# A four-stage local attention layer on one core: three groups of matmuls in another place of TensorE's order

## The chip, the cores and the metric

The kernel runs on one core of one Trainium2 chip. The metric is the device time of one execution in microseconds. A core has five engines that run their own instruction streams and meet through semaphores: TensorE (PE in the profile, with its weight loads as PEld), VectorE (DVE), ScalarE (ACT), GpSimd (POOL) and SyncE (SP), which issues the DMAs.

## What is computed

The reference is `x + attention(xn) * silu(ffn(xn))` on 4096 tokens of 256 features, with `xn` the normalised input. The change lies in the second branch, which applies two layers of this kind (cut to its attention half; each layer then has a gated MLP):

```python
h = shift_token(x)                       # second half of the features from the token before
q, k, v = split(h @ wqkv)                # 8 heads of 64
q = l2norm(q) * qs;  k = l2norm(k) * ksc
q, k = rotary_xpos(q, k)                 # rotation with a position-dependent scale
o = local_attention(q, k, v)             # windows of 128, each sees itself and the one before
x = x + o @ wo
```

## The kernel before, in words

The program goes through stages one after the other: projection and global attention (to about 1700 us of the trace), its output product, then for each of two layers `local_attention_layer` and `mlp_layer`, and a final gate. Only `local_attention_layer` is touched. It runs twice, the first time from about 1745 to 2312 us of the trace, the second from about 2581 to 3149 us.

**The pipeline.** The 32 windows are taken in 16 pairs (`NI = 16`). Every engine runs the same loop `for k in range(NI + 4)`, and in iteration k works on pairs of different age; `live(k)` is true for the pairs 0 to 15, `win(w)` for the windows 0 to 31. The order inside an iteration is written out by hand on every engine. Since each engine executes in its own order, an instruction that waits holds all behind it on that engine. Iterations 4 to 15 have all work; iterations 16 to 19 are the drain, in which nothing new is projected.

On PE one iteration of before is, in this order (lines of the profile):

- `score_max(2k-3)` (L1142): scores of a window, from which DVE takes the row maxima (`row_max`, L1350, eight custom reductions of 128x256)
- transposes of X for pair k (L1260)
- `weigh(k-4, 1)` (L1245): the softmax weights PT times V, and times ones for the sums, heads 4 to 7; DVE then divides (`divide`: reciprocal L1382, product L1386), ACT copies the high part (L1071), POOL takes the low part (L992)
- `score_turned(2k-5)` (L1159 for the maxima, L1166 for the scores): the transposed scores, of which ACT makes exponentials (L1043, `weights`), and POOL cuts the corners (L1001, L1005, `trim`)
- transposes of the norm factors (L1276), which DVE multiplies into the rotated q and k of pair k-1 (L1420)
- `turn_max(2k-3)` (L1180): the maxima transposed into bank B7, copied by ACT to `negm` (L1051)
- `values(2k)` (L76 to L78 into B6): 6 matmuls of 512 columns; ACT copies them to V (L1058)
- **the output product of pair k-4** (L76 to L78 with `a_woh`, `a_oTh`, also into B6): 24 matmuls of 256 columns; DVE adds it to X (L1428)
- `project(k, 0)` and `project(k, 1)` (L76 to L78 into BP): 12 matmuls each; ACT squares them (L1064), DVE rotates them (`turn`, L1376)
- `score_max(2k-2)`, `project(k, 2)`, `project(k, 3)`, `values(2k+1)`, `score_turned(2k-4)`
- sums of squares into B6 (L1313), copied by ACT to `sse` (L1117)
- `turn_max(2k-2)` (L1180)
- **the sums of squares transposed** (L1321, two transposes into B6); DVE takes them (L1440, `ssc`), POOL raises them to the power -1/2 (L1026), ACT spreads them (L1096, `rnx`)
- `weigh(k-3, 0)` (L1245): heads 0 to 3 of the pair before.

`product3` writes each fp32 product as three matmuls of high and low parts, which is why the lines L76, L77 and L78 come in turn.

**Buffers that tie the order.** B6 is shared by the value products, the output product, the sums of squares and the sums of `weigh(p, 1)`; B7 by the transposed maxima, the transposes of X and the sums of `weigh(p, 0)`. So `weigh(p, 0)` waits until ACT has copied the maxima out of B7, and `weigh(p, 1)` waits until DVE has read the output product before it and `ssc` out of B6:

```python
                if q == 0:
                    ...
                    pe.wait_ge(nm_done, min(2 * k - 1, NT))
                else:
                    pe.wait_ge(ssc_done, min(k + 1, NI))
                    if p >= 1:
                        pe.wait_ge(x2_done, p)
```

## Time and profile before

| | |
|---|---|
| median of 3 runs | 3445.2 us (3440.74 to 3447.95) |
| profiled execution, its own time | 3442.12 us |
| span of that execution | 3440.4 us |
| mean granted TensorE clock | 0.954 of full speed |
| PE busy | 3080.8 us (90% of the span) |
| PEld busy | 1909.2 us (55%) |
| DVE busy | 2413.1 us (70%) |
| ACT busy | 1714.0 us (50%) |
| POOL busy | 953.9 us (28%) |
| first local layer's iterations | about 1745 to 2312 us of the span |
| second local layer's iterations | about 2581 to 3149 us of the span |

A row of a timeline gives the start in us from the span's start, the duration in us, the engine, the line and operation, what is written and read, and how many instructions were merged. In square brackets stands how long the engine was idle before it and what ended that. Merged matmuls overlap their neighbours, since they are pipelined; the distance between starts tells more than a duration. The PEclk column is the granted clock of TensorE, where 1.00 is 2.4 GHz and 0.50 is 1.2 GHz.

### The profile page before, as it was taken

How to read it: one execution, taken by the hardware profiler on the slowest of the kernel's cores; microseconds unless marked ns; L12 is line 12 of the kernel's file. 1: busy time of each engine (PE TensorE's matmuls, PEld its weight loads, DVE VectorE, ACT ScalarE, POOL GpSimd, SP SyncE). 2: the span in 40 equal slices, each digit the busy share in tenths (PEclk: the TensorE clock that was granted, in tenths of full speed). 3: DMA queues.
4: the chain of work that ended last, by engine and by line, in shares of the span. 5: the costliest groups of instructions: out<-in, count | busy, mean ns of one | idle time of the engine just before them, and what ended most of it. 6: DMA issues, size and time to landing. Idle time of an engine off the chain costs nothing. (4 is left out here: it accounts for less than half of the span.)

```text
span 3440.4 us, 77045 instructions
## 1 busy us (share of the span) xinstructions
PE 3080.8 (90%) x31756; PEld 1909.2 (55%) x31756; DVE 2413.1 (70%) x4236; ACT 1714.0 (50%) x3173; POOL 953.9 (28%) x1011
## 2 busy tenths in 40 slices
PE   7799999999999999999868998968987999986996
PEld 6333333334443333434457777757876777765875
DVE  7699999987889997875246666645555666664555
ACT  5267777887778888887223333322223333332222
POOL 8410000000110000001035545532224555542223
PEclk9699999999999999999789999989998999998998
DMA  8420001000020000000220000000000000003001
GB/s 255 127 63 17 9 9 46 9 9 18 25 69 17 9 9 10 5 8 8 73 91 20 20 14 20 32 28 6 0 5 31 20 16 19 20 26 112 0 0 49
DMA packets 61014, 113.91 MB, mean 33 GB/s; under 512 B 9240, under 2 KB 25368, under 8 KB 60056
## 3 DMA queue, kind: packets, MB, share of 16 engines
q1 hardware_dynamic: 56600, 103.07, 9.6%
q10 hardware_dynamic: 4096, 6.30, 0.7%
q8 instruction: 236, 3.87, 0.5%
q14 instruction: 82, 0.67, 0.1%
HBM read 75.00 MB, written 33.55 MB: 32 GB/s over the span
## 5 line engine op out<-in xcount | busy, mean ns | idle before, releaser
L650 DVE TENSOR_REDUCE mp<-ps_m 128x2 f32<-128x1024 f32 (+3 forms) x1152 | 1275.8, 1134 | 192.5 <-PE ps_m L701 134.8
L628 ACT ACTIVATE probs<-ps_s 128x512 f32<-128x512 f32 (+3 forms) x2304 | 1162.1, 561 | 380.5 <-PE ps_s L725 349.7
L741 PE MATMUL ps_o<-probs,vall 128*32 128x256 f32 (+3 forms) x9216 | 711.1, 380 | 15.4 <-POOL probs L605 9.1
L725 PE MATMUL ps_s<-qst,kst 64*128 64x512 f32 (+3 forms) x2304 | 595.7, 486 | 4.3 <-ACT probs L628 2.9
L701 PE MATMUL ps_m<-kst,qst 64*128 64x512 f32 (+3 forms) x2304 | 481.3, 401 | 33.1 <-DVE mp L650 15.7
L725 PEld LDWEIGHTS ps_s<-qst,kst 64*128 64x128 f32 x2304 | 241.3, 187 | 459.3 <-ACT probs L628 398.9
L741 PEld LDWEIGHTS ps_o<-probs,vall 128*32 128x32 f32 x9216 | 186.0, 109 | 342.1 <-issue 177.0
L701 PEld LDWEIGHTS ps_m<-kst,qst 64*128 64x128 f32 x2304 | 233.3, 192 | 77.1 <-DVE mp L650 57.8
L594 POOL TENSOR_TENSOR msplit<-negm,mzero 128x16 fp32r<-128x16 f32 x32 | 7.2, 224 | 907.0 <-DVE negm L656 907.0
L1020 POOL TENSOR_TENSOR a_rot<-a_scr 128x512 f32<-128x512 f32 x128 | 163.4, 1277 | 321.3 <-DVE a_scr L1376 321.3
L605 POOL TENSOR_SCALAR_AFFINE_SELECT probs<-probs 128x256 f32<-128x256 f32 x256 | 103.0, 406 | 513.0 <-ACT probs L628 512.9
L1554 ACT ACTIVATE m_gl<-m_bank_u,m_b 128x512 f32<-128x512 f32 x96 | 66.0, 688 | 346.7 <-PE m_bank_u L78 346.7
L1376 DVE SCALAR_TENSOR_TENSOR a_scr<-a_BP,a_sc,a_tab 128x256 f32<-128x256 f32 x384 | 167.5, 478 | 63.5 <-ACT a_scr L1064 63.2
L1064 ACT ACTIVATE a_scr<-a_BP 128x512 f32<-128x512 f32 x128 | 76.5, 598 | 266.7 <-PE a_BP L78 266.7
L1350 DVE CUSTOM_DVE_ANT_0 a_SU<-a_SU,a_mask 128x256 f32<-128x256 f32 (+1 forms) x512 | 196.5, 459 | 9.8 <-issue 9.8
L1071 ACT ACTIVATE a_oTh<-a_on 128x512 fp32r<-128x512 f32 x64 | 40.4, 631 | 317.0 <-DVE a_on L1386 317.0
L1026 POOL TENSOR_TENSOR a_rn<-a_ssc,a_half 128x32 f32<-128x32 f32 x32 | 174.1, 5441 | 40.5 <-DVE a_ssc L1440 40.5
L76 PE MATMUL m_bank_u<-m_hh,Wh 128*128 128x512 f32 x384 | 155.7, 405 | 31.5 <-DVE m_uf L1663 31.5
L1382 DVE RECIPROCAL a_rec<-a_B 128x256 f32<-128x256 f32 x64 | 112.2, 1753 | 98.3 <-PE a_B L1245 98.1
L1537 POOL TENSOR_TENSOR m_ul<-m_uf,m_uh 128x512 fp32r<-128x512 f32 x96 | 126.2, 1314 | 195.4 <-DVE m_uh L1669 195.4
L1043 ACT ACTIVATE a_PT<-a_SU 128x1024 f32<-128x1024 f32 (+1 forms) x128 | 121.8, 1003 | 89.2 <-PE a_SU L1166 89.2
L78 PE MATMUL m_bank_u<-m_hh,Wl 128*128 128x512 f32 x384 | 152.9, 398 | 0.0
(189 smaller groups left out, 5411.7 us busy)
## 6 DMA issues: line engine op xcount, KB each, us to landing
a_tab<-in_rope SPq DMA_DIRECT2D x32, 512.0 KB
q_parts<-pparts SPq DMA_DIRECT2D x32, 256.0 KB, 3.6
k_parts<-pparts SPq DMA_DIRECT2D x32, 256.0 KB, 3.9
qst<-q_parts SPq DMA_DIRECT2D x64, 128.0 KB, 2.7
o_raw<-o_sb SPq DMA_DIRECT2D x32, 256.0 KB, 2.0
X<-in_x SPq DMA_DIRECT2D x8, 512.0 KB, 5.7
kst<-k_parts SPq DMA_DIRECT2D x32, 128.0 KB, 3.7
qst<-q_parts SPq DMA_DIRECT2D x64, 64.0 KB, 2.6
```

What stands on the lines that cost most here:

```text
L76: pe.matmul(out, a_hi, b_hi, start=start, stop=False)
L78: return pe.matmul(out, a_lo, b_hi, start=False, stop=stop)
L628: act.activation(probs[:, s % PR, h, off:C], sslots[n % SR][:, off:C], ACT.Exp, scale=float(D) ** -0.5).then_inc(exp_done, 1)
L650: dve.tensor_reduce(mp[b % 2][:, h:h + 2, cc:cc + 1], slot[:, :, 0:width], AX.X, ALU.max).then_inc(max_read, 1)
L701: last = pe.matmul(slot[:, x, 0:width], qst[q_slot(b)][rows, hp, a * P:(a + 1) * P], kst[g % 2][rows, hp, cc * C:cc * C + width], start=Tr ...
L725: pe.matmul(sslots[n % SR][:, off:C], kst[g % 2][rows, hp, i * P:(i + 1) * P], qst[q_slot(b)][rows, hp, off:C], start=True, stop=True).the ...
L741: last = pe.matmul(ps_o[32 * h:32 * h + VW, lo:hi], vall[:, i, (g * GH + h) * DV:(g * GH + h) * DV + VW], probs[:, s % PR, h, lo:hi], star ...
L1020: pool.tensor_tensor(rot[:, g, :, :].rearrange("p a b -> p (a b)"), t[:, n % 2, 0, :, :].rearrange("p a b -> p (a b)"), t[:, n % 2, 1, :, ...
L1026: pool.tensor_tensor(rn[:, :, :, :].rearrange("p a b c -> p (a b c)"), ssc[:, :, :, :].rearrange("p a b c -> p (a b c)"), half[:, :], ALU. ...
L1350: dve.tensor_tensor_reduce(SU[:, i, q * N2 + lo:(q + 1) * N2], SU[:, i, q * N2 + lo:(q + 1) * N2], mask[:, lo:N2], 1.0, -3.0e38, ALU.add, ...
L1376: dve.scalar_tensor_tensor(out=dst, in0=src, scalar=s, in1=table, op0=ALU.mult, op1=ALU.mult).then_inc(rope_done, 1)
L1537: pool.tensor_tensor(u_lo[:, m, :], uf[:, m % 2, :], u_hi[:, m, :].bitcast(F32), ALU.subtract).then_inc(ul_done, 1)
```

## The change

Three groups are moved; no instruction is added or removed, and no wait is changed but by its place.

1. **Output product in the iterations that project** (k = 4 to 15): on PE it moves from behind `values(2k)` to behind `project(k, 0)`. Its code becomes the helper `project_out(p)`. DVE's order stays.
2. **Sums of squares transposed**: the two transposes (L1321) move from before `weigh(k-3, 0)` to behind it. DVE's order stays: `ssc`, then the division of `weigh(k-3, 0)`.
3. **Output product in the drain** (k = 16 to 19): on PE it moves from the middle of the iteration to its end, behind `weigh(k-3, 0)`; on DVE the addition to X moves to the end of the iteration, behind `divide(k-3, 0)`.

```diff
--- before.py
+++ after.py
@@ -1247,6 +1247,21 @@
                                              tile_position=(0, 32 * i), skip_group_check=True)
                 last.then_inc(av_done, 1)
 
+            def project_out(p):
+                if live(p):
+                    if p == 0:
+                        pe.wait_ge(wl_done, 1)
+                    pe.wait_ge(olo_done, 2 * p + 2)
+                    pe.wait_ge(rec_done, 2 * p + 2)
+                    if live(p + 4):
+                        pe.wait_ge(vc_done, 2 * (p + 4) + 1)
+                    for a in range(2):
+                        tok = slice(a * P, (a + 1) * P)
+                        for j in range(OC):
+                            last = product3(pe, B6[:, a * E:(a + 1) * E], oT_hi[:, j, tok], oT_lo[:, j, tok], wo_hi[:, j, :],
+                                            wo_lo[:, j, :], j == 0, j == OC - 1)
+                    last.then_inc(wo_done, 1)
+
             for k in range(NI + 4):
                 if win(2 * k - 3):
                     score_max(2 * k - 3)
@@ -1280,22 +1295,9 @@
                     turn_max(2 * k - 3)
                 if live(k):
                     values(2 * k)
-                if live(k - 4):
-                    p = k - 4
-                    if p == 0:
-                        pe.wait_ge(wl_done, 1)
-                    pe.wait_ge(olo_done, 2 * p + 2)
-                    pe.wait_ge(rec_done, 2 * p + 2)
-                    if live(k):
-                        pe.wait_ge(vc_done, 2 * k + 1)
-                    for a in range(2):
-                        tok = slice(a * P, (a + 1) * P)
-                        for j in range(OC):
-                            last = product3(pe, B6[:, a * E:(a + 1) * E], oT_hi[:, j, tok], oT_lo[:, j, tok], wo_hi[:, j, :],
-                                            wo_lo[:, j, :], j == 0, j == OC - 1)
-                    last.then_inc(wo_done, 1)
                 if live(k):
                     project(k, 0)
+                    project_out(k - 4)
                     project(k, 1)
                 if win(2 * k - 2):
                     score_max(2 * k - 2)
@@ -1315,13 +1317,15 @@
                     last.then_inc(ss_done, 1)
                 if win(2 * k - 2):
                     turn_max(2 * k - 2)
+                if live(k - 3):
+                    weigh(k - 3, 0)
                 if live(k):
                     pe.wait_ge(sse_done, k + 1)
                     for a in range(2):
                         last = pe.transpose(B6[:, a * P:(a + 1) * P], sse[:, a * P:(a + 1) * P], id_sb[:, :])
                     last.then_inc(sst_done, 1)
-                if live(k - 3):
-                    weigh(k - 3, 0)
+                else:
+                    project_out(k - 4)
 
         @block.vector
         def _(dve):
@@ -1386,6 +1390,12 @@
                     dve.tensor_tensor(on[:, 2 * q:2 * q + 2, :], BP[q][:, :, :],
                                       rec[:, q, :].rearrange("p (o n) -> p o n", o=1).broadcast_to([P, 2, N2]), ALU.mult
                                       ).then_inc(on_done, 1)
+
+            def add_out(p):
+                if live(p):
+                    dve.wait_ge(wo_done, p + 1)
+                    xt = X[:, 2 * p:2 * p + 2, :].rearrange("p a e -> p (a e)")
+                    dve.tensor_tensor(xt, B6[:, :], xt, ALU.add).then_inc(x2_done, 1)
 
             for k in range(NI + 4):
                 if k == 1:
@@ -1421,12 +1431,8 @@
                                           rot[:, 2 * b:2 * b + 2, :, :],
                                           BP[b][:, :, :].rearrange("p g (o n) -> p g o n", o=1).broadcast_to([P, 2, 2, N2]),
                                           ALU.mult).then_inc(nrm_done, 1)
-                if live(k - 4):
-                    p = k - 4
-                    dve.wait_ge(wo_done, p + 1)
-                    xt = X[:, 2 * p:2 * p + 2, :].rearrange("p a e -> p (a e)")
-                    dve.tensor_tensor(xt, B6[:, :], xt, ALU.add).then_inc(x2_done, 1)
-                if live(k):
+                if live(k):
+                    add_out(k - 4)
                     turn(k, 0)
                     turn(k, 1)
                 if win(2 * k - 2):
@@ -1440,6 +1446,8 @@
                     dve.tensor_scalar(ssc[:, :, :, :], B6[:, 0:N2].rearrange("p (a g c) -> p a g c", a=2, g=4)[:, :, :, 0:4],
                                       1e-24, None, ALU.max).then_inc(ssc_done, 1)
                 divide(k - 3, 0)
+                if not live(k):
+                    add_out(k - 4)
 
 
 def mlp_layer(nc, layer, X, W, w_next, ahead, w_2, b_1, ln_cols, b_2, ident, shift, carry):
```

How the orders differ at three places; the names are those of the profile, with the buffer's number where it tells two apart.

PE, first iteration with an output product, from the value product (into B6, operand `Wh`, `a0_hTh`) on. Before, the output product (`a0_woh`, `a0_oTh`) follows:

```order
L76 MATMUL a0_B6<-Wh,a0_hTh 128x512
L77 MATMUL a0_B6<-Wl,a0_hTh 128x512
L78 MATMUL a0_B6<-Wh,a0_hTl 128x512
L76 MATMUL a0_B6<-a0_woh,a0_oTh 128x256
L77 MATMUL a0_B6<-a0_wol,a0_oTh 128x256
L78 MATMUL a0_B6<-a0_woh,a0_oTl 128x256
```

With the change the quarter of the projection (into BP0) comes first; its last three rows and the output product's first three:

```order
L76 MATMUL a0_BP0<-a0_hTh,Wh 128x256
L77 MATMUL a0_BP0<-a0_hTl,Wh 128x256
L78 MATMUL a0_BP0<-a0_hTh,Wl 128x256
L76 MATMUL a0_B6<-a0_woh,a0_oTh 128x256
L77 MATMUL a0_B6<-a0_wol,a0_oTh 128x256
L78 MATMUL a0_B6<-a0_woh,a0_oTl 128x256
```

The 24 matmuls of the output product stand one quarter, 12 matmuls, later than before.

PE, end of an iteration. Before: maxima transposed, sums of squares transposed (`a0_sse`), weighting (`a0_PT`), scores of the next iteration (`a0_SU`):

```order
L1180 MATMUL a0_B7<-a0_id,a0_msp 128x128 x2
L1321 MATMUL a0_B6<-a0_id,a0_sse 128x128 x2
L1245 MATMUL a0_BP0<-a0_PT,a0_V 32x128 x4
L1245 MATMUL a0_BP0<-a0_PT,a0_V 32x256 x4
L1245 MATMUL a0_BP0<-a0_PT,a0_V 32x128 x8
L1245 MATMUL a0_BP0<-a0_PT,a0_V 32x256 x4
L1245 MATMUL a0_BP0<-a0_PT,a0_V 32x128 x4
L1245 MATMUL a0_B7<-a0_PT,a0_ones 32x128 x4
L1245 MATMUL a0_B7<-a0_PT,a0_ones 32x256 x4
L1245 MATMUL a0_B7<-a0_PT,a0_ones 32x128 x4
L1142 MATMUL a0_SU<-a0_QK 128x256 x16
```

With the change:

```order
L1180 MATMUL a0_B7<-a0_id,a0_msp 128x128 x2
L1245 MATMUL a0_BP0<-a0_PT,a0_V 32x128 x4
L1245 MATMUL a0_BP0<-a0_PT,a0_V 32x256 x4
L1245 MATMUL a0_BP0<-a0_PT,a0_V 32x128 x8
L1245 MATMUL a0_BP0<-a0_PT,a0_V 32x256 x4
L1245 MATMUL a0_BP0<-a0_PT,a0_V 32x128 x4
L1245 MATMUL a0_B7<-a0_PT,a0_ones 32x128 x4
L1245 MATMUL a0_B7<-a0_PT,a0_ones 32x256 x4
L1245 MATMUL a0_B7<-a0_PT,a0_ones 32x128 x4
L1325 MATMUL a0_B6<-a0_id,a0_sse 128x128 x2
L1142 MATMUL a0_SU<-a0_QK 128x256 x16
```

The two transposes now stand behind the whole weighting and before the next scores (the trace counts 72 matmuls of a weighting, where these rows add up to 36).

DVE, drain, iterations 17 and 18 from the division of `weigh(13, 1)` on (`Wl` is the low part of the MLP's weights). Before:

```order
L1382 RECIPROCAL a_rec<-a_B 128x256
L1386 TENSOR_TENSOR a_on<-a_BP,a_rec 128x512
L1428 TENSOR_TENSOR X<-a_B,X 128x512
L1382 RECIPROCAL a_rec<-a_B 128x256
L1386 TENSOR_TENSOR a_on<-a_BP,a_rec 128x512
L1397 TENSOR_TENSOR Wl<-a_scr,Wh 128x3072
L1382 RECIPROCAL a_rec<-a_B 128x256
L1386 TENSOR_TENSOR a_on<-a_BP,a_rec 128x512
L1428 TENSOR_TENSOR X<-a_B,X 128x512
```

With the change:

```order
L1386 RECIPROCAL a_rec<-a_B 128x256
L1390 TENSOR_TENSOR a_on<-a_BP,a_rec 128x512
L1386 RECIPROCAL a_rec<-a_B 128x256
L1390 TENSOR_TENSOR a_on<-a_BP,a_rec 128x512
L1398 TENSOR_TENSOR X<-a_B,X 128x512
L1407 TENSOR_TENSOR Wl<-a_scr,Wh 128x3072
L1386 RECIPROCAL a_rec<-a_B 128x256
L1390 TENSOR_TENSOR a_on<-a_BP,a_rec 128x512
L1386 RECIPROCAL a_rec<-a_B 128x256
L1390 TENSOR_TENSOR a_on<-a_BP,a_rec 128x512
L1398 TENSOR_TENSOR X<-a_B,X 128x512
```

The addition to X now follows the second division of its iteration, and `Wl` follows it directly.

## Rows read from the trace of the kernel before

**Rows 1.** Windows of the first local layer, steady part and drain; busy us, then PEclk
```profile
1850.00:2250.00 400.00, 363.06 (x5410) 295.31 (x5410) 265.30 (x770) 132.32 (x218) 218.42 (x187) 1.00 0.07 20
2250.00:2313.00 63.00, 42.66 (x764) 35.27 (x756) 26.80 (x54) 13.65 (x17) 18.28 (x20) 0.86 0.01 2
```
**Rows 2.** Waits of PE over the whole span: total us, times, longest
```profile
PE a_B L1321 <- ACT a_sse L1117: 28.3, 30, 1.0
...
PE a_B L76 <- POOL a_oTl L992: 28.0, 8, 6.3
...
PE a_B L76 <- ACT a_V L1058: 25.7, 24, 1.1
```
**Rows 3.** Timeline of PE, one pair in the steady part: start us, duration us, what
```profile
2049.17 0.40 PE L78 MATMUL a_B<-Wh,a_hTl 128*128 128x512 f32 x1
...
2050.64 0.35 PE L76 MATMUL a_B<-a_woh,a_oTh 128*128 128x256 f32 x1 [1.07 <-ACT a_V L1058]
...
2053.56 0.28 PE L76 MATMUL a_BP<-a_hTh,Wh 128*128 128x256 f32 x1
...
2056.53 2.07 PE L1142 MATMUL a_SU<-a_QK 32*128 32x128 f32 x64
```
**Rows 4.** Timeline of DVE, the same stretch
```profile
2053.76 0.69 DVE L1428 TENSOR_TENSOR X<-a_B,X 128x512 f32<-128x512 f32 x1 [4.26 <-PE a_B L78]
```
**Rows 5.** Timeline of ACT, the same pair and the start of the next
```profile
2049.89 0.61 ACT L1058 ACTIVATE a_V<-a_B 128x512 f32<-128x512 f32 x1
...
2067.61 0.41 ACT L1051 ACTIVATE a_negm<-a_B 128x256 fp32r<-128x256 f32 x1
...
2074.66 1.04 ACT L1096 ACTIVATE a_rnx<-a_rn 128x1024 f32<-128x1024 f32 x1
```
**Rows 6.** Timeline of PE, end of that pair
```profile
2067.79 0.44 PE L1321 MATMUL a_B<-a_id,a_sse 128*128 128x128 f32 x2 [0.97 <-ACT a_sse L1117]
...
2068.16 1.94 PE L1245 MATMUL a_BP<-a_PT,a_V 128*32 128x128 f32 x48
...
2070.90 2.01 PE L1142 MATMUL a_SU<-a_QK 32*128 32x256 f32 x32
```
**Rows 7.** Timeline of ACT, then of PE, end of the first drain iteration
```profile
2259.98 0.39 ACT L1051 ACTIVATE a_negm<-a_B 128x256 fp32r<-128x256 f32 x1
...
2260.51 1.94 PE L1245 MATMUL a_BP<-a_PT,a_V 128*32 128x128 f32 x48 [1.81 <-ACT a_negm L1051]
```
**Rows 8.** Timeline of DVE, end of that pair
```profile
2068.27 0.19 DVE L1440 TENSOR_SCALAR a_ssc<-a_B 128x32 f32<-128x32 f32 x1 [2.57 <-PE a_B L1321]
...
2071.04 1.76 DVE L1382 RECIPROCAL a_rec<-a_B 128x256 f32<-128x256 f32 x1 [2.58 <-PE a_B L1245]
```
**Rows 9.** Timeline of PE, first part of the next pair
```profile
2076.66 0.44 PE L1159 MATMUL a_SU<-a_negm,a_rowso 32*128 32x128 f32 x8 [0.41 <-DVE a_mx L1350]
...
2079.10 0.66 PE L1276 MATMUL a_BP<-a_id,a_rnx 128*128 128x128 f32 x4
```
**Rows 10.** Timeline of POOL, the same stretch
```profile
2068.54 5.45 POOL L1026 TENSOR_TENSOR a_rn<-a_ssc,a_half 128x32 f32<-128x32 f32 x1 [1.49 <-DVE a_ssc L1440]
```
**Rows 11.** Timeline of PE, last three iterations of the first local layer
```profile
2279.20 1.95 PE L1245 MATMUL a_BP<-a_PT,a_V 128*32 128x128 f32 x48
...
2292.28 0.58 PE L76 MATMUL a_B<-a_woh,a_oTh 128*128 128x256 f32 x1 [6.34 <-POOL a_oTl L992]
...
2297.22 1.95 PE L1245 MATMUL a_BP<-a_PT,a_V 128*32 128x128 f32 x48
...
2299.85 1.92 PE L1245 MATMUL a_BP<-a_PT,a_V 128*32 128x128 f32 x48
```
**Rows 12.** Timeline of POOL, the same iterations
```profile
2276.66 0.63 POOL L1005 TENSOR_SCALAR_AFFINE_SELECT a_PT<-a_PT 128x512 f32<-128x512 f32 x1
...
2293.36 1.22 POOL L1001 TENSOR_SCALAR_AFFINE_SELECT a_PT<-a_PT 128x512 f32<-128x512 f32 x2
```
**Rows 13.** Timeline of DVE, the same iterations
```profile
2284.49 3.35 DVE L1397 TENSOR_TENSOR Wl<-a_scr,Wh 128x3072 fp32r<-128x3072 f32 x1
```

## The prediction

> **What bounds the kernel now.** I first looked at the windows, to see whether the touched stage is short of TensorE or of something else. In the steady part of the first local layer PE is busy 363 of 400 us at full clock, while DVE has 265 and the others less; in the drain PE is busy 42.7 of 63 us, at a mean clock of 0.86 [rows 1]. So in the steady part time is gained by closing holes in PE, and in the drain by shortening chains. The list of PE's waits names the holes that the change aims at: 25.7 us in 24 waits of the output product for ACT's copy of the values, 28.3 us in 30 waits of the turned sums of squares for ACT's `sse`, 28.0 us in 8 waits of the output product for POOL's low part [rows 2]. Taken at their names that is 82 us. The timelines, read next, show that only the first is what it seems. Both layers run the same instructions at the same distances, so I count one and double.
>
> **Part 1, the output product behind a quarter of the projection.** The last value matmul starts at 2049.17, the output product at 2050.64 after 1.07 us of idleness, the projection at 2053.56, the next scores at 2056.53 [rows 3]. The product thus takes 2.92 us and a quarter of the projection 1.49 (half of 2.97). The quarter needs neither B6 nor ACT's copy, so it starts when the values end, some 0.3 us after 2049.17. It ends at about 2050.9, the copy at 2049.89 + 0.61 = 2050.50 [rows 5], so the product no longer waits. The scores then start 0.3 + 1.49 + 2.92 + 1.49 = 6.2 us after 2049.17 instead of 7.36: 1.2 us earlier. Does DVE allow it? Its addition to X starts at 2053.76, 0.20 behind the product's end [rows 4], and comes 0.2 to 0.3 us later now; but the rotation behind it, which had to wait for the first quarter's squares, finds them ready, and starts over 1 us earlier. Iterations 4 to 15 of two layers are 24 cases: 24 x 1.2 = 28.8 us less. Bounds: the printed idleness alone gives 25.7, a start without any gap 29.5.
>
> **Part 2, the turned sums of squares behind the weighting.** PE idles 0.97 us before these transposes (2067.79), and the weighting follows at 2068.16 [rows 6]. That wait looks free to take. But the weighting writes its sums into B7 and so needs ACT's copy of the maxima, which runs from 2067.61 to 2068.02 [rows 5]. The weighting starts 0.14 us after that. In the drain, where nothing stands between, the copy ends at 2260.37 and the weighting starts at 2260.51, again 0.14 later [rows 7]. So the weighting is held by the copy already, will start at the same time, and the idleness before it only grows from 0.97 to about 1.34 us. Gain: nothing. The cost: the transposes now stand at the weighting's end, where the next scores started, 2070.90 [rows 6]. PE's scores move back by 0.37 (2067.79 to 2068.16). DVE took `ssc` 0.48 us after the transposes' start, at 2068.27, and started the reciprocal at 2071.04 [rows 8]. Now `ssc` starts at 2070.90 + 0.48 = 2071.38, lasts 0.19, and the reciprocal, queued behind it on DVE, starts at about 2071.55: 0.5 us later. Behind it are the product, eight maxima and their split; PE waits for exactly these at 2076.66, by 0.41 us [rows 9]. DVE sets the pace there, so 0.5 us is paid in full. The weighting of a pair and the projection of a new one fall together in iterations 3 to 15, twice: 26 x 0.5 = 13.0 us more. Bounds: 0.37 each (PE's share alone) gives 9.6, 0.48 + 0.19 = 0.67 each gives 17.4. One more queue has to bear it: POOL's power -1/2, 5.45 us long, started 0.27 us after `ssc` [rows 10] and comes 3.1 us later, to end at 2077.1; ACT's spreading (1.04 us, [rows 5]) ends at 2078.2. PE wants it at 2079.10 + 0.5 [rows 9]. That leaves 1.4 us of slack: cost nothing.
>
> Here the clock has to be looked at. In the steady part holes of 1.07 and 0.97 us recur in every iteration, and the granted clock stays at 1.00 [rows 1, 3, 6]; so a hole of 1.34 us instead of 0.97, with the 1.07 gone, is costed at nothing. The Trainium skill (TensorE: Matmul & The Clock Gate, section on HAM oscillation) says that matmul groups separated by waits can each start at the low clock, every time anew. By that rule the sum would be some 50 us higher (worked out below as a rival), and I do not take it, since this trace holds its clock through such holes.
>
> **Part 3, the drain.** Before, the output product waits up to 6.34 us for the low part, then runs from 2292.28 to 2297.22, 4.94 us instead of 2.92 because PE idled before it: the low clock costs 2.0 us [rows 3, 11]. Moving it behind the weighting hides these waits, but `weigh(p, 1)` of the next iteration may only start when the addition to X has emptied B6, and this now stands behind weighting and product in a line. Followed through: the weighting of pair 14 is held by POOL's trims, which end at 2277.29, so it starts at 2277.4 instead of 2279.20 [rows 11, 12]. Weighting 2.74, product 2.92, addition 0.20 + 0.69: done at 2284.0. Only then comes `Wl` on DVE, 3.35 us [rows 13], done at 2287.3 where it was 2287.84: the chain division, high part, low part, trims behind it gains 0.5 us, and the weighting of pair 15, which waits for the trims (before: to 2294.58, [rows 12]), starts at 2294.1 instead of 2297.22 [rows 11]. PE has idled for 6 us by then, so I give the weighting 2.74 + 2.0. Product and addition: 2302.7. Then `weigh(15, 1)` starts, where before it started at 2299.85. From there the chain to the layer's end is as before. The drain gets longer by 2.8 us per layer, 5.6 together. The first two drain iterations give back what they gain, since the product that leaves one row of scores comes before the next. Bounds: 0 per layer, if the weighting keeps the full clock and some gain survives; 5, if one more burst falls to the low clock.
>
> **Sum.** -28.8 + 13.0 + 5.6 = -10.2 us. The profiled execution took 3442.1 us and would take 3431.9. The median of the runs is 3445.2, 3.1 above it, so the prediction is 3435.0. The ends: -29.5 + 9.6 + 0 = -19.9 gives 3425.3; -25.7 + 17.4 + 10 = +1.7 gives 3446.9.
>
> **The rivals.**
> - *The wait for `sse` does vanish.* Then the weighting starts 1.3 us earlier, the reciprocal 0.8: -28.8 - 26 x 0.8 + 5.6 = -44, 3401 us. For it speaks the list of waits, which names `sse` 28.3 us; against it the 0.14 us in both places [rows 5 to 7]. 0.03.
> - *The drain gains.* The last product of a layer keeps its wait; if the other six lose theirs and nothing takes their place, 28.0 x 6/8 = 21 us go: -28.8 + 13.0 - 21 = -36.8, 3408 us. Against it speaks the wait on `x2_done`. 0.06.
> - *The norm factors come late.* If POOL's power ends later than I make it, by trims or low parts before it in its queue, PE waits at L1276. It decides from 1.4 us of further delay; each 0.1 us beyond costs 2.6 us in 26 cases. With 0.3 us it is 3443. 0.10.
> - *The clock falls before the weighting, and the kernel gets slower.* The place is the hole of 1.34 us in front of L1245. A burst at 1.2 GHz costs 2.0 us more (4.94 against 2.92). In all 26 cases: 3435 + 52 = 3487 us; from 5 bursts on the gain is gone, from 9 on the kernel is slower by over 0.2%. This is the rule of the Trainium skill named above (TensorE: Matmul & The Clock Gate). 0.05.
> - *The value copy is not covered after all*, with only some 0.3 us between its end and the product's new place, or the drain is worse than its bound: 3440 to 3450. 0.04.
>
> **Chances and range.** The forecast's own case has 0.72, spread over 3427 to 3443. A measurement of this kernel can tell about 0.2% (6.9 us) from no change. Faster by more, below 3438.3: 0.60 of the forecast's 0.72, the two fast rivals (0.09) and 0.02 of the third, 0.71. Within: 0.11 of the forecast, 0.07 of the third rival and 0.03 of the last, 0.21. Slower: 0.01 of the forecast, 0.05 of the clock and 0.02 of the others, 0.08. The range 3422 to 3443 leaves out the two fast rivals (0.09), the clock, and a few hundredths at the upper end.
>
> **What would show it.** In the profile after: no wait of the output product for `a_V`, the next scores 6.2 us after the last value matmul. PE idle about 1.3 us before the weighting, released by `negm` (L1051), still 0.14 us behind its end; `ssc` and the reciprocal adjacent on DVE, the latter 3.4 us after the weighting's start where it was 2.9. The distance of equal points in neighbouring iterations 0.7 us shorter than before. In the drain the 6.34 us wait for POOL gone, but `weigh(15, 1)` waiting for the addition to X, and the layer's last addition some 3 us later counted from the last `sse`. I am wrong if the weighting starts earlier relative to the copy, if L1276 waits for `rnx` in the steady part, or if the clock there leaves 1.00.

## The result, and the profile after

The median of 15 runs is 3454.3 us (3448.7 to 3463.0), that of the kernel before, run beside it, 3440.8: a ratio of 1.0043 with an interval of 1.0033 to 1.0052. The change makes the kernel 13.5 us slower, which is more than the 6.9 us that the prediction called measurable, and the time lies above the predicted range of 3422 to 3443 us. The profiled execution is the slowest of the fifteen, 3463.0 us, 20.9 above the profiled one of before.

The list of PE's waits (total us, times, longest) shows that the waits which the change aims at did go:

```profile
PE a_BP L1245 <- ACT a_negm L1051: 39.0, 28, 2.1
PE a_BP L1291 <- DVE a_on L1390: 31.5, 26, 1.3
...
PE a_BP L1245 <- POOL a_PT L1001: 12.2, 2, 6.1
...
PE a_B L76 <- POOL a_oTl L992: 9.2, 2, 4.6
...
PE a_SU L1159 <- ACT a_negm L1051: 5.6, 2, 2.8
...
PE a_BP L1245 <- DVE X L1398: 3.5, 4, 0.9
...
PE a_B L1325 <- ACT a_sse L1117: 2.9, 4, 1.0
```

The 25.7 us for `a_V` are gone from the output product, the 28.3 us for `sse` have shrunk to 2.9, the 28.0 us for POOL's low part to 9.2 [rows 2]. In their place stand 39.0 us of the weighting for `negm`, 31.5 us of the spread norm factors for DVE's `a_on` (11.5 us in the list of before), and in the drain 12.2 us for POOL's trims and 3.5 us for the addition to X, which the prediction foresaw, and 5.6 us of the turned scores for `negm`, which it did not. `a_on` comes late since DVE does: by 0.45 us for the reciprocal, and by the splits shown below. The PE timeline of the same pair as before (start us, duration us, what, idle time before it and its releaser):

```profile
2048.00 0.66 PE L1291 MATMUL a_BP<-a_id,a_rnx 128*128 128x128 f32 x4 [1.27 <-DVE a_on L1390]
...
2049.87 0.40 PE L78 MATMUL a_B<-Wh,a_hTl 128*128 128x512 f32 x1
...
2051.55 0.28 PE L76 MATMUL a_B<-a_woh,a_oTh 128*128 128x256 f32 x1
...
2055.90 2.07 PE L1142 MATMUL a_SU<-a_QK 32*128 32x128 f32 x64
...
2067.53 1.94 PE L1245 MATMUL a_BP<-a_PT,a_V 128*32 128x128 f32 x48 [1.34 <-ACT a_negm L1051]
...
2070.27 0.44 PE L1325 MATMUL a_B<-a_id,a_sse 128*128 128x128 f32 x2
...
2076.47 0.44 PE L1159 MATMUL a_SU<-a_negm,a_rowso 32*128 32x128 f32 x8 [0.41 <-DVE a_mx L1354]
```

From the last value matmul to the scores pass 6.03 us where it was 7.36 [rows 3]: Part 1 works. The weighting has 1.34 us of idleness before it, released by `negm`, as forecast. On ACT that copy is:

```profile
2066.98 0.40 ACT L1051 ACTIVATE a_negm<-a_B 128x256 fp32r<-128x256 f32 x1
```

It ends at 2067.38 and the weighting starts 0.15 us later, where rows 5 to 7 have 0.14. DVE and POOL show what was not forecast. First DVE:

```profile
2070.75 0.19 DVE L1446 TENSOR_SCALAR a_ssc<-a_B 128x32 f32<-128x32 f32 x1 [5.72 <-PE a_B L1325]
2070.86 1.75 DVE L1386 RECIPROCAL a_rec<-a_B 128x256 f32<-128x256 f32 x1
...
2076.45 0.65 DVE L1361 TENSOR_SCALAR a_msp<-a_mx 128x8 fp32r<-128x8 f32 x1
2077.14 0.55 DVE L1363 SCALAR_TENSOR_TENSOR a_msp<-a_mx,a_msp 128x8 fp32r<-128x8 f32 x1
```

and POOL in the same stretch:

```profile
2071.02 5.45 POOL L1026 TENSOR_TENSOR a_rn<-a_ssc,a_half 128x32 f32<-128x32 f32 x1 [4.63 <-DVE a_ssc L1446]
2076.43 0.64 POOL L1001 TENSOR_SCALAR_AFFINE_SELECT a_PT<-a_PT 128x512 f32<-128x512 f32 x1
2077.02 0.64 POOL L1005 TENSOR_SCALAR_AFFINE_SELECT a_PT<-a_PT 128x512 f32<-128x512 f32 x1
```

The two small DVE instructions that split the maxima of a row took 0.18 and 0.17 us before:

```profile
2076.64 0.18 DVE L1357 TENSOR_SCALAR a_msp<-a_mx 128x8 fp32r<-128x8 f32 x1
2076.86 0.17 DVE L1359 SCALAR_TENSOR_TENSOR a_msp<-a_mx,a_msp 128x8 fp32r<-128x8 f32 x1
```

Now they start 0.02 and 0.12 us behind the start of one of POOL's two trims, and each ends 0.03 us behind that trim's end (2077.10 against 2077.07, 2077.69 against 2077.66). Before, POOL was past both trims by then:

```profile
2073.95 0.64 POOL L1001 TENSOR_SCALAR_AFFINE_SELECT a_PT<-a_PT 128x512 f32<-128x512 f32 x1
2074.54 0.63 POOL L1005 TENSOR_SCALAR_AFFINE_SELECT a_PT<-a_PT 128x512 f32<-128x512 f32 x1
2075.14 1.28 POOL L992 TENSOR_TENSOR a_oTl<-a_on,a_oTh 128x512 fp32r<-128x512 f32 x1
```

POOL was done with all three at 2076.42, before the first split began at 2076.64.

The drain, from ACT's last copy of `sse` to DVE's last addition to X, in the first layer, for before and then for after (window, its length, busy us of PE, PE loads, DVE, ACT, POOL with instructions, PEclk, DMA share, GB/s):

```profile
2230.93:2311.70 80.77, 59.14 (x1080) 48.89 (x1080) 37.59 (x81) 18.64 (x26) 30.93 (x31) 0.89 0.06 22
```
```profile
2229.98:2321.63 91.65, 66.31 (x1080) 54.20 (x1080) 38.31 (x81) 18.75 (x26) 31.66 (x31) 0.83 0.05 19
```

It takes 10.9 us more (10.7 in the second layer), and for the same 1080 matmuls PE is busy 7.2 us more, at a mean clock of 0.83 instead of 0.89. For one layer the difference of the two profiled executions adds up like this: from the first `sse` to the fourth +1.0 us (75.7 to 76.8; this distance moves between 74.8 and 77.5 over both layers of all kernels run here, for a reason not looked into), the twelve iterations behind it -1.4 (392.8 to 391.4), the drain +10.8. That is 10.4, and twice that is 20.8.

In the table below a period is the distance of ACT's `sse` copies over ten iterations of the first layer, and the drains are the windows just named, first and second layer. A, B and C stand for Parts 1, 2 and 3.

| kernel | median, us | against before | ratio, interval | period | drains |
|---|---|---|---|---|---|
| before | | | | 32.76 | 80.8, 80.9 |
| changed (A, B, C) | 3454.3 | +13.5 | 1.0043 (1.0033 to 1.0052) | 32.67 | 91.7, 91.6 |
| a_only | 3407.6 | -34.3 | 0.9897 (0.988 to 0.9913) | 31.46 | 80.9, 79.7 |
| b_only | 3470.2 | +28.3 | 1.0079 (1.0064 to 1.0094) | 33.99 | 83.7, 83.6 |
| c_only | 3446.9 | +5.0 | 1.001 (0.9995 to 1.0026) | 32.76 | 86.9, 84.3 |
| ab | 3442.7 | +1.3 | 1.0005 (0.9991 to 1.002) | 32.67 | 84.2, 85.0 |
| ac | 3417.5 | -23.6 | 0.9928 (0.9902 to 0.9954) | 31.46 | 87.6, 88.8 |
| bc | 3484.5 | +43.1 | 1.0132 (1.011 to 1.0154) | 33.99 | 89.4, 87.8 |
| b_held | 3449.9 | +8.1 | 1.0026 (1.0013 to 1.0038) | 33.20 | 82.6, 81.3 |
| ab_held | 3423.6 | -17.5 | 0.9946 (0.9927 to 0.9965) | 31.89 | 81.3, 83.5 |
| a_mid | 3393.8 | -47.6 | 0.9868 (0.9846 to 0.989) | 31.46 | 76.4, 76.6 |
| a_drain | 3389.6 | -51.8 | 0.9852 (0.9829 to 0.9875) | 31.46 | 72.9, 72.8 |
| a_max | 3394.9 | -48.6 | 0.9866 (0.9843 to 0.9889) | 31.67 | 72.0, 72.6 |
| ab_max | 3351.7 | -89.4 | 0.9741 (0.9714 to 0.9768) | 30.19 | 71.1, 71.2 |

"Against before" is the difference between the kernel's median and that of before in the same series (3441.1 to 3443.4 us), both without the few runs in the slow state.

Two measures of one change stand in this table, and they do not always agree. Periods and drains come from one profiled execution. c_only shows how far apart the two can be: its two drains together are 9.5 us longer than before's, and yet its profiled execution took 3442.8 us, like before's 3442.1. Its first `sse`, ahead of everything that was changed, came at 1753.3 us where before's came at 1762.4. In the fourteen profiled executions this point lies between 1748.4 and 1762.4, though the code ahead of it is the same. So differences of a few us between medians of 5 to 12 runs have to be read with their intervals. The periods, each a mean over ten iterations, agree within 0.04 us between the two layers.

### The profile page after: what moved, and what is told of

Same layout as the page of the kernel before. It is cut to its first block and busy times, and to the rows that moved or that the text cites. A ratio compares the mean times of both kernels' runs of the same rounds, so it can differ in the third digit from the quotient of the medians.

```text
span 3461.2 us, 77045 instructions
## 1 busy us (share of the span) xinstructions
PE 3089.3 (89%) x31756; PEld 1927.9 (56%) x31756; DVE 2433.3 (70%) x4236; ACT 1717.9 (50%) x3173; POOL 957.1 (28%) x1011
## 5 line engine op out<-in xcount | busy, mean ns | idle before, releaser
L1562 ACT ACTIVATE m_gl<-m_bank_u,m_b 128x512 f32<-128x512 f32 x96 | 66.3, 690 | 347.9 <-PE m_bank_u L78 347.9
L1064 ACT ACTIVATE a_scr<-a_BP 128x512 f32<-128x512 f32 x128 | 76.6, 598 | 234.6 <-PE a_BP L78 234.6
L1245 PE MATMUL a_BP<-a_PT,a_V 128*32 128x256 f32 (+1 forms) x3008 | 129.8, 323 | 54.8 <-ACT a_negm L1051 39.0
```

The costliest lines, as they stand in the source:

```text
L1245: last = pe.matmul(out, v, PT[:, kb % PR, i, q * N2 + pc:q * N2 + pc + n], start=(d != 1 and j == 0), stop=(j == len(parts) - 1), tile_pos ...
```

## The experiments

**Each part alone.** Diffs are against the changed kernel; each takes two of the three parts back. The output product alone:

```diff
@@ a_only, PE @@
                     project_out(k - 4)
                     project(k, 1)
+                else:
+                    project_out(k - 4)
...
-                if live(k - 3):
-                    weigh(k - 3, 0)
                 if live(k):
                     pe.wait_ge(sse_done, k + 1)
...
                     last.then_inc(sst_done, 1)
-                else:
-                    project_out(k - 4)
+                if live(k - 3):
+                    weigh(k - 3, 0)
```

On DVE `add_out(k - 4)` has one place, where it stood before.

> Only the output product of iterations 4 to 15 is moved behind project(k, 0); the turned sums of squares and the drain are as before. Theory 1 (from the trace of the changed kernel, where the distance from the last value matmul to the next scores fell from 7.36 to 6.03 us): 24 x 1.33 = 32 us faster than before. Theory 2 (the forecast's term): 24 x 1.2 = 29 us faster. Rival (the gain was eaten elsewhere in the steady part, so the move is worth nothing): within 7 us of before. The distance between equal points of neighbouring iterations should fall from 32.86 to 31.5 us.

Measured: -34.3 us, the period 1.31 us shorter. 24 x 1.31 = 31.4 us, some 3 less than the difference of the medians and inside its interval. The small splits keep 0.18 and 0.17. The transposes behind the weighting alone:

```diff
@@ b_only, PE @@
                 if live(k):
-                    project(k, 0)
                     project_out(k - 4)
+                    project(k, 0)
                     project(k, 1)
+                else:
+                    project_out(k - 4)
...
                     last.then_inc(sst_done, 1)
-                else:
-                    project_out(k - 4)
```

> Only the two transposes of the sums of squares are moved behind weigh(k-3, 0). Theory 1 (the weighting is held by the copy of the maxima, the reciprocal starts 0.45 us later behind ssc, and the two small DVE instructions that split the maxima lose another 0.82 us because POOL's later work now runs beside them): 26 x 1.27 = 33 us slower. Theory 2 (the forecast's term, without the small instructions): 13 us slower. Rival (the wait for sse vanishes): 21 us faster.

On DVE `add_out(k - 4)` stands as in a_only.

Measured: +28.3 us, over twice the +13 of the prediction, and a period longer by 1.23 us where the prediction had 0.5 and Theory 1 had 1.27. The first split on DVE and the first trim on POOL, in b_only as in the changed kernel:

```profile
2079.09 0.65 DVE L1361 TENSOR_SCALAR a_msp<-a_mx 128x8 fp32r<-128x8 f32 x1
```
```profile
2079.07 0.64 POOL L1001 TENSOR_SCALAR_AFFINE_SELECT a_PT<-a_PT 128x512 f32<-128x512 f32 x1
```

Part 2 alone brings the longer splits. ACT's spreading `rnx` begins in the same moment as the trims do, so which of the two slows DVE is open at this point.

The drain's product alone:

```diff
@@ c_only, PE @@
                 if live(k):
-                    project(k, 0)
                     project_out(k - 4)
+                    project(k, 0)
...
-                if live(k - 3):
-                    weigh(k - 3, 0)
                 if live(k):
                     pe.wait_ge(sse_done, k + 1)
...
                     last.then_inc(sst_done, 1)
-                else:
+                if live(k - 3):
+                    weigh(k - 3, 0)
+                if not live(k):
                     project_out(k - 4)
```

> Only the drain is changed: output product and addition to X at the end of iterations 16 to 19. Theory 1 (weigh(p, 1) stands behind weighting, product and addition, and PE idles more, so that more matmuls run at 1.2 GHz): 10 to 22 us slower; the distance from the layer's last sse transposes to its last addition to X grows by 5 to 11 us per layer. Theory 2 (the forecast's term): 5.6 us slower. Rival (the drain gains): up to 21 us faster.

Measured: +5.0 us, with an interval that reaches from slightly faster to slower, beside the prediction's +5.6. By the median that is Theory 2; by the drains, 6.1 and 3.4 us longer than before's, it is no less Theory 1's 5 to 11 us in the first layer. Its two drains differ by 2.6 us (86.9 and 84.3, at mean clocks of 0.84 and 0.88), though both run the same instructions.

**Whether POOL's trims lengthen DVE's splits.** Against b_only, POOL gets one wait more, behind the power, so that the trims come after the splits. ACT's spreading stays where it is, since it waits for the power alone.

```diff
@@ b_held, POOL, behind the power -1/2 @@
+                    if k >= 3:
+                        pool.wait_ge(ml_done, 2 * k)
```

> As the run with only the transposes moved, and POOL waits behind its power -1/2, in iterations 3 to 15, until DVE has split the maxima of the next window (ml_done), so that POOL's trims do not run beside the two small DVE instructions; ACT's spreading of the norm factors still starts at the same time. Theory 1 (POOL and DVE get in each other's way): the two instructions take 0.17 us again instead of 0.65 and 0.55, and the time is 12 us above before, 21 below the run without the hold. Rival (ACT's spreading is what slows DVE, or the small instructions cost nothing on the path): they stay at 0.65 and 0.55, or the time stays as without the hold.

Measured: +8.1 us, 20.2 less than b_only, and a period of 33.20: 0.44 above before, which is the forecast of Part 2, and 0.79 below b_only. The rows of DVE, of POOL and of ACT:

```profile
2073.55 0.18 DVE L1363 TENSOR_SCALAR a_msp<-a_mx 128x8 fp32r<-128x8 f32 x1
```
```profile
2074.01 0.64 POOL L1001 TENSOR_SCALAR_AFFINE_SELECT a_PT<-a_PT 128x512 f32<-128x512 f32 x1 [0.44 <-DVE a_msp L1365]
```
```profile
2073.60 1.06 ACT L1098 ACTIVATE a_rnx<-a_rn 128x1024 f32<-128x1024 f32 x1 [1.93 <-POOL a_rn L1026]
```

ACT's spreading starts 0.05 us behind the first split and covers the whole second one (2073.76 to 2073.93), and both are short again; only the trims moved. That settles it: POOL is the cause, not ACT. Of the 128 splits of both layers 52, which is 26 pairs, take over 0.3 us in the changed kernel, in b_only and in ab; in b_held and ab_held none does. Over the whole kernel the groups of the two splits, of the changed kernel (lines L1361 and L1363) and of b_held (L1363 and L1365), read:

```profile
L1361 DVE TENSOR_SCALAR a_msp<-a_mx 128x8 fp32r<-128x8 f32 x64 | 23.4, 366 | 2.2
L1363 DVE SCALAR_TENSOR_TENSOR a_msp<-a_mx,a_msp 128x8 fp32r<-128x8 f32 x64 | 21.0, 327 | 2.2
```
```profile
L1363 DVE TENSOR_SCALAR a_msp<-a_mx 128x8 fp32r<-128x8 f32 x64 | 11.2, 175 | 2.2
L1365 DVE SCALAR_TENSOR_TENSOR a_msp<-a_mx,a_msp 128x8 fp32r<-128x8 f32 x64 | 11.2, 175 | 2.2
```

44.4 against 22.4 us: 22.0 us, which is 26 pairs of splits at 0.85 (0.47 + 0.38), and about the gap between b_only and b_held.

**Whether the parts add.** The three pairs:

```diff
@@ ab, PE @@
                     project(k, 1)
+                else:
+                    project_out(k - 4)
...
                     last.then_inc(sst_done, 1)
-                else:
-                    project_out(k - 4)
@@ ac, PE @@
-                if live(k - 3):
-                    weigh(k - 3, 0)
...
                     last.then_inc(sst_done, 1)
-                else:
+                if live(k - 3):
+                    weigh(k - 3, 0)
+                if not live(k):
                     project_out(k - 4)
@@ bc, PE @@
-                    project(k, 0)
                     project_out(k - 4)
+                    project(k, 0)
```

> Output product behind the first projection quarter and transposes behind the weighting together, drain as before. Theory 1 (the parts add, and what is missing in the sum of the three single runs, -34 + 28 + 5 = -1 against the measured +13.5, comes from the drain): 6 us faster than before, steady distance 32.67 us as in the full change, drain of each layer 1 to 3 us longer than before's 80.8. Rival (the two parts disturb each other in the steady part): 8 us slower.

> Output product behind the first projection quarter and the new drain, transposes as before. Theory 1 (the new drain is costly above all where the late transposes of the last pair come with it: it cost 5 us alone, 13 with them): 26 to 30 us faster than before, drain 84 to 87 us per layer. Rival (the drain is costlier beside the moved output product): 17 to 21 us faster, drain about 91 us as in the full change.

> Transposes behind the weighting and the new drain, without the move of the output product in the steady part. Theory 1 (the late transposes of the last pair push the drain into more stretches at 1.2 GHz; the two parts are worse together than alone): 40 to 48 us slower than before, drain 90 us or more per layer. Rival (they add): 33 us slower, drain about 87 to 89 us.

Measured: +1.3, -23.6 and +43.1 us. In the steady part the parts add: A shortens the period by 1.31 and B lengthens it by 1.23; together 32.67 where that sum gives 32.68. In the drain they do not add, but how far they miss depends on the measure. By the medians Part 3 costs 5.0 us alone, 10.7 beside A (ac less a_only), 14.8 beside B (bc less b_only) and 12.2 beside both (changed kernel less ab). By the two drains of the profiled executions it costs 9.5, 15.8, 9.9 and 14.2 us. Both measures have it dearer beside A and beside both; beside B alone they contradict each other, so that is not shown. The sum of the single parts is -34.3 + 28.3 + 5.0 = -1.0 us, against 13.5 measured. ac lies between its theory (26 to 30 us faster) and its rival (17 to 21) and does not decide between them.

The same pair with POOL's wait:

```diff
@@ ab_held against ab, POOL, behind the power -1/2 @@
+                    if k >= 3:
+                        pool.wait_ge(ml_done, 2 * k)
```

> Output product behind the first projection quarter, transposes behind the weighting, POOL held behind its power -1/2 until DVE has split the maxima; drain as before. Theory 1 (POOL beside the two small DVE instructions costs 0.8 us in each of 26 iterations): 20 us faster than the two moves without the hold, 3422 us, steady distance 31.9 us. Rival (with the shorter iteration the held POOL becomes late, or the hold pays only without the moved product): within 7 us of the two moves without it.

Measured: -17.5 us, 18.8 less than ab, the period 0.78 us shorter: the collision costs the same in A's company. It also shows that B is a loss without the collision, by 16.8 us against a_only.

**What the drain's product costs by its place.** In these two, the product of the drain stands behind `score_max(2k-2)`, so that it fills a stretch in which PE otherwise waits for DVE's maxima; the second also makes the next layer's `Wh` and `Wl` two and one iterations earlier, off the last chain.

```diff
@@ a_mid against a_only, PE @@
-                else:
-                    project_out(k - 4)
                 if win(2 * k - 2):
                     score_max(2 * k - 2)
+                if not live(k):
+                    project_out(k - 4)
@@ a_mid against a_only, DVE @@
                     row_max(2 * k - 2)
+                if not live(k):
+                    add_out(k - 4)
@@ a_drain against a_mid, ACT @@
-                if k == NI + 1:
+                if k == NI:
                     act.wait_ge(next_in, 16)
                     act.wait_ge(v_done, NT)
                     act.activation(W[0][:, :], scr[:, 0:WCOLS], ACT.Copy).then_inc(next_high, 1)
@@ a_drain against a_mid, DVE @@
-                if k == NI + 2:
+                if k == NI:
                     dve.wait_ge(next_high, 1)
...
```

The pieces of a_drain are shown at one place, but they move: the piece on ACT stands behind `turn_max(2k-3)`, the one on DVE ahead of `divide(k-3, 0)`.

> Output product behind the first projection quarter; in the drain it stands behind score_max(2k-2), and DVE's addition to X behind row_max(2k-2), so that in iteration 16 it fills the hole in which PE waits for the maxima; transposes as before. Theory 1: 2.5 us per layer faster than the move of the output product alone, for the 3.3 us hole filled, and up to 2 more where the low clock is avoided: 39 to 43 us faster than before. Rival (the drain is set by another chain): 34 us faster, as the move alone.

> As the run before, and the high and low parts of the MLP's weights are made in iteration 16 (ACT behind the first turned maxima, DVE behind the second row maxima) instead of 17 and 18, so that the 3.35 us of Wl no longer stand before the reciprocal of weigh(14, 1). Theory 1: another 3 us per layer, 45 to 49 us faster than before. Rival (Wl was off the path, or the weights have not landed by then): as the run before, or slower.

Measured: -47.6 and -51.8 us, both more than Theory 1 had. The drain of a_mid is 4.4 us shorter than before's in the first layer and 4.3 in the second, that of a_drain by another 3.5 and 3.9. The first layer's window in a_drain:

```profile
2206.75:2279.61 72.86, 56.54 (x1080) 47.04 (x1080) 37.59 (x81) 18.64 (x26) 29.04 (x31) 0.95 0.07 24
```

The mean clock is 0.95 and PE is busy 2.6 us less than before, 9.8 less than in the changed kernel, for the same matmuls. POOL's sum is 1.9 us shorter as well (the last section shows the row).

**What keeps Part 2 from paying.** If the copy `negm` holds the weighting, it has to be moved first. In ab_max PE transposes the row's maxima ahead of `score_turned(2k-4)`, and ACT copies them ahead of the exponentials of that row.

```diff
@@ ab_max against a_drain, PE @@
+                if win(2 * k - 2):
+                    turn_max(2 * k - 2)
                 if win(2 * k - 4):
                     score_turned(2 * k - 4)
...
-                if win(2 * k - 2):
-                    turn_max(2 * k - 2)
+                if live(k - 3):
+                    weigh(k - 3, 0)
...
-                if live(k - 3):
-                    weigh(k - 3, 0)
@@ ab_max against a_drain, POOL, behind the power -1/2 @@
+                    if k >= 3:
+                        pool.wait_ge(ml_done, 2 * k)
```

a_max is ab_max without the move of `weigh(k-3, 0)` and without POOL's wait.

> The kernel with the new middle drain and the early weights (the fastest so far), and with it the transposes behind the weighting, POOL held, and turn_max(2k-2) on PE ahead of score_turned(2k-4) and on ACT ahead of weights(2k-4), so that the copy of the maxima no longer holds the weighting. Theory 1 (the copy is what holds it): the weighting starts 1.36 us earlier, the reciprocal 1.36 - 0.45 = 0.9, so 26 x 0.9 = 23 us faster than the fastest so far, about 3366 us. Rival (the weighting is then held by another wait, or DVE or POOL come late): no faster, or up to 12 us slower from the 0.45 us.

> As the fastest so far (3352 us), but with the transposes of the sums of squares ahead of the weighting again and POOL not held; the copy of the maxima stays early. Theory 1 (the weighting has two holders that end almost together, the copy of the maxima and, through the transposes, the copy of the sums of squares; taking away one gives nothing): steady distance 31.46 us as with the output product's move alone, 3390 us, the same as without the early copy. Rival (the early copy alone makes the gain, and where the transposes stand does not matter): about 3352 us, distance 30.2 us.

Measured: ab_max -89.4 us, a_max -48.6. ab_max came out at 3351.7 us where its Theory 1 had 3366. On PE of ab_max the weighting follows the sums of squares (L1321) with no idleness between:

```profile
2036.82 1.07 PE L1321 MATMUL a_B<-a_scr,a_blocks 128*32 128x256 f32 x16
2037.70 1.92 PE L1247 MATMUL a_BP<-a_PT,a_V 128*32 128x128 f32 x48
...
2040.42 0.44 PE L1329 MATMUL a_B<-a_id,a_sse 128*128 128x128 f32 x2
```

while in a_max the transposes still stand ahead of it and wait, longer than before:

```profile
2053.90 0.44 PE L1325 MATMUL a_B<-a_id,a_sse 128*128 128x128 f32 x2 [1.35 <-ACT a_sse L1123]
```

The early copy alone gains nothing: the period is even 0.21 longer than a_drain's. The transposes of the maxima, 0.32 us, used to lie inside PE's wait for `sse`, and now stand ahead of the scores on which that wait hangs; from those scores (L1159) to the weighting it is 5.15 us in a_max and 5.16 in a_drain, so what was taken out of the hole is added in front of it. That gives the direction, not the exact 0.21. Part 2 alone does nothing for the weighting either. Both together, with POOL's wait, shorten the period by 1.27 us: two holders ended within 0.3 us of each other, `sse` and `negm`, and both had to go. How much of the 1.27 is due to POOL's wait was not run; without the early copy it shortened the period by 0.79 us beside B and by 0.78 beside A and B. ab_max is the best version here, faster than before by 2.6% and than the changed kernel by some 100 us.

## Why the prediction was wrong

It said 3435.0 (3422 to 3443), with 0.08 on slower; it was 3454.3. The forecast difference was -10.2 us and the measured one is +13.5, so the sum is off by 23.7 us. Of these, 4.4 do not show in the forecast time, by luck: the median of before, its starting point, was 3445.2 us in three runs and 3440.8 in fifteen. The steady distance was to become 0.7 us shorter and became 0.09 shorter.

**Part 1, right.** Forecast 1.2 us per iteration, measured 1.33 on PE and 1.31 in the period. a_only gives 34.3 us where 28.8 were forecast, 2.6 of the difference by the size of the step (24 x 0.11).

**Part 2, the forecast mechanism right, and a term missing.** That the weighting stays held by `negm` was seen (39.0 us now under its name), and so was the price: weighting to reciprocal 2.88 us before [rows 6, 8], 3.33 after, the period of b_held 0.44 longer against 0.5 forecast. The idleness of 1.34 us left the clock of the steady part alone: it is 1.00 from 1850 to 2230 us of the changed kernel, so that rival falls. What failed is the sentence on POOL: "That leaves 1.4 us of slack: cost nothing." It asked only who waits for the power's result, and PE at L1291 indeed did not wait for `rnx` there. It did not ask what else POOL has in its queue behind a power that comes 3.1 us later, and what DVE does in that moment. The trims moved from 2073.95 to 2076.43, onto DVE's splits. They cost 0.78 us of every period, some 20 us in all (b_only less b_held 20.2, ab less ab_held 18.8). With it the sum of the prediction would have been +10, near the 13.5 measured. That closeness is partly luck: Part 1 gained 2.6 us more than its term, while the drains of the profiled pair cost 21.6 us where 5.6 stood. The trace of before had already shown the effect, once per layer and near its start: in the first layer a first split of 0.44 us at 1846.78, ending 0.03 us behind POOL's low part of 1845.92 (1.27 us long).

**Part 3, the sign right, the size off.** Forecast 2.8 us per layer. The drain of the changed kernel is 10.9 longer in the first layer; b_only's is 2.9 longer without Part 3, which the forecast did not have either. PE of the first layer's drain, after:

```profile
2245.91 3.49 PE L1142 MATMUL a_SU<-a_QK 32*128 32x128 f32 x64 [1.66 <-ACT a_PT L1043]
...
2259.25 3.02 PE L1245 MATMUL a_BP<-a_PT,a_V 128*32 128x128 f32 x48 [2.07 <-ACT a_negm L1051]
...
2266.69 2.01 PE L1142 MATMUL a_SU<-a_QK 32*128 32x256 f32 x32
...
2274.42 0.44 PE L1180 MATMUL a_B<-a_id,a_msp 128*128 128x128 f32 x2
2277.65 0.69 PE L1159 MATMUL a_SU<-a_negm,a_rowso 32*128 32x128 f32 x8 [2.79 <-ACT a_negm L1051]
...
2282.22 2.71 PE L1245 MATMUL a_BP<-a_PT,a_V 128*32 128x128 f32 x48
...
2299.92 3.64 PE L1245 MATMUL a_BP<-a_PT,a_V 128*32 128x128 f32 x48 [6.10 <-POOL a_PT L1001]
...
2308.75 1.94 PE L1245 MATMUL a_BP<-a_PT,a_V 128*32 128x128 f32 x48 [0.88 <-DVE X L1398]
```

and before:

```profile
2248.08 2.07 PE L1142 MATMUL a_SU<-a_QK 32*128 32x128 f32 x64
...
2263.26 2.01 PE L1142 MATMUL a_SU<-a_QK 32*128 32x256 f32 x32
...
2271.44 0.44 PE L1180 MATMUL a_B<-a_id,a_msp 128*128 128x128 f32 x2
2273.82 0.38 PE L76 MATMUL a_B<-a_woh,a_oTh 128*128 128x256 f32 x1 [1.94 <-POOL a_oTl L992]
...
2276.83 0.45 PE L1159 MATMUL a_SU<-a_negm,a_rowso 32*128 32x128 f32 x8
```

To lay them side by side, 0.95 us is added to the times of after, since its last `sse` came that much earlier. How late PE then is:

| point of PE's program | before | after + 0.95 | late by |
|---|---|---|---|
| `score_max(30)`, iteration 16 (L1142) | 2248.08 | 2246.86 | -1.2 |
| `weigh(13, 0)` (before: rows 7) | 2260.51 | 2260.20 | -0.3 |
| `score_max(31)`, iteration 17 (L1142) | 2263.26 | 2267.64 | 4.4 |
| `turn_max(31)` (L1180) | 2271.44 | 2275.37 | 3.9 |
| `score_turned(30)` (L1159) | 2276.83 | 2278.60 | 1.8 |
| `weigh(14, 0)` (before: rows 11) | 2279.20 | 2283.17 | 4.0 |
| `weigh(15, 0)` (before: rows 11) | 2297.22 | 2300.87 | 3.7 |
| `weigh(15, 1)` (before: rows 11) | 2299.85 | 2309.70 | 9.9 |
| last addition to X (DVE) | 2311.70 | 2322.58 | 10.9 |

Two statements of mine failed. "The first two drain iterations give back what they gain": iteration 16 gained 1.2 us, not the 4.1 of product and wait, since its scores now wait 1.66 us for ACT's exponentials, and it lost that by 1.4 us of low clock (3.49 against 2.07). Iteration 17 starts with a weighting at the low clock (3.02 against 1.94, and more in its sums) and with a product of 3.02 us ahead of the next scores: 4.7 us. The other statement is "so it starts at 2277.4 instead of 2279.20", of the weighting of pair 14: I took POOL's trims as its only holder. `score_turned(30)` stands ahead of it in PE's queue and needs ACT's copy of the maxima that `turn_max(31)` turned. Before, the product lay in that latency; taking it out gave back only 2.1 us, left a hole of 2.79, and behind the hole the 2.37 us from L1159 to the weighting became 4.57. So this weighting came 4.0 us late where I had it 1.8 early: 5.8 of the 8.1 us by which the forecast of this layer was short. Another 1.0 went between it and pair 15's (17.7 us, forecast 16.7), and 1.0 behind the last weighting. The step between was right: the second half 8.8 us behind the first (forecast 8.6), held by the addition to X, with the first at the low clock (3.64).

Why Part 3 costs more in company than alone stays open. The longer drains mostly have the lower mean clock (c_only 0.84 and 0.88, ac 0.85, changed 0.83, before 0.89), but bc's second has 0.89 and is 87.8 us long, and c_only's two drains of equal instructions differ by 2.6 us. Part 2 also makes PE later before the drain's first scores (its maxima are turned 1.3 us late, 2243.87 + 0.95 against 2243.56), so that Part 3's holes fall on a longer chain. Which small shift tips a burst to the low clock was not isolated, and the 7 us between the profiled difference (20.9) and that of the medians (13.5) is not accounted for either. One hole is followed by both levels: PE waits 1.66 us for the exponentials ahead of `score_max(30)` in the changed kernel and in a_drain, and where the row of the changed kernel above has 3.49 us (clock 0.55), that of a_drain has full speed:

```profile
2221.41 2.07 PE L1142 MATMUL a_SU<-a_QK 32*128 32x128 f32 x64 [1.66 <-ACT a_PT L1043]
```

**The rivals.** "The wait for `sse` does vanish" came true in its name alone (28.3 to 2.9 us): the weighting still starts 0.15 us behind `negm`. "The norm factors come late" looked at the right instruction and at the wrong party: PE never waited for them, DVE's splits paid. "The drain gains" is refuted for this place of the product, and true for another one (a_mid: 8.7 us in the drains of two layers). The last rival, with 0.04, named a drain worse than its bound of 5 us per layer; that is what came, with 10.9 and 10.7.

## What to carry to other kernels

When an instruction of POOL moves, everything behind it in its queue moves too: lay the new times of that queue beside DVE's queue, and look for small SBUF-to-SBUF operations of DVE that it now meets, before giving the shift no cost. Look first for instructions whose duration varies at one line and shape: the trace of before had a split of 0.44 us among those of 0.18. A wait that two instructions end almost together (here 0.3 us apart) gives nothing until both are moved, so find the second before costing the first. In a drain, work in the right place is cover: a product is better put into a stretch where PE waits for another engine (a_mid) than behind the last weighting, since a hole there can be paid twice, once as idleness and once as low clock.

## What the runs showed of the hardware

**DVE and POOL block each other in SBUF.** A `TENSOR_SCALAR` and a `SCALAR_TENSOR_TENSOR` of 128x8, SBUF to SBUF, took 0.18 and 0.17 us alone and 0.65 and 0.55 us beside a trim of POOL that had started 0.02 and 0.12 us earlier, ending 0.03 us after it in each case. The Trainium skill has the rule in SBUF — State Buffer, "Who interferes with whom": one port pair is shared by VectorE and GpSimd, held for a whole instruction by whichever starts first, and wanted by VectorE for `tensor_scalar` in its two-port mode and for operations with two inputs in SBUF. The trace agrees in the endings, which follow POOL's end and not the size of the operation. It agrees the other way round as well: POOL's low part (L992), 1.26 to 1.31 us elsewhere, takes 4.31 us beside DVE's `Wl`, which started 0.16 us earlier and has two SBUF inputs:

```profile
2289.62 4.31 POOL L992 TENSOR_TENSOR a_oTl<-a_on,a_oTh 128x512 fp32r<-128x512 f32 x1 [4.95 <-ACT a_oTh L1071]
```
```profile
2289.46 3.35 DVE L1407 TENSOR_TENSOR Wl<-a_scr,Wh 128x3072 fp32r<-128x3072 f32 x1
```

`Wl` ends at 2292.81 and POOL's low part at 2293.93, 1.12 us later: most of its own length behind the end of the block. The kernel before has the same beside its `Wl` [rows 13], with a later start and so a shorter block; it ends at 2288.95, 1.11 us behind the end of `Wl`:

```profile
2285.31 3.64 POOL L992 TENSOR_TENSOR a_oTl<-a_on,a_oTh 128x512 fp32r<-128x512 f32 x1 [3.65 <-ACT a_oTh L1071]
```

In a_drain, where `Wl` stands away from it, none of the 64 low parts takes over 1.31 us. Which of its modes VectorE took for the `TENSOR_SCALAR`, no run here shows. The same blocking on DVE's side is the largest term missing from my sum.

**The clock in the drain.** A hole of 1.34 us in every period of the steady part left it at full speed, while in the changed kernel's drain, with holes of up to 6.1 us, PE was busy 66.3 us at a mean clock of 0.83. In a_drain's drain, with holes of up to 4.6 us, the same 1080 matmuls took 56.5 us at 0.95. Between two kernels that differ in order alone, 9.8 us per layer of PE's busy time came and went. The length of a hole alone does not tell which level follows: after the same 1.66 us, 64 matmuls of scores took 3.49 us in one kernel and 2.07 in the other.
